# Gated expert values turned by VectorE and memory instead of TensorE, and a peeled step in a new order

## The reference, cut to what matters

```python
# x: (64 sequences, 64 heads, 1024 samples), float32; lengths and languages: one number for each sequence
mask = arange(1024) < length[:, None]
kernel = 2 * real(einsum('hn,hnl->hl', Cs, exp(dtA[:, :, None] * arange(1024))))   # a filter for each head
y = irfft(rfft(x * mask, 2048) * rfft(kernel, 2048))[..., :1024]                   # causal convolution
x = x + (y + x * mask * D[:, None]) * mask

base = einsum('btd,od->bto', x, W)                       # d = o = 1024; t is the head, b the sequence
logits = einsum('btd,ed->bte', x, Wr) + 5 * one_hot(language)       # 8 experts
topw, topi = top_k(logits, 2); gates = softmax weights of the two, put at their experts
h = einsum('btd,erd->bter', x, A)                        # rank 16: 8 x 16 = 128 values for each token
x = x + base + 2 * einsum('bter,bte,eor->bto', h, gates, B)
```

## Time and profile before

| | |
|---|---|
| median of 3 runs (lowest to highest) | 632.15 us (630.82 to 632.97) |
| the profiled execution's own time, its span | 630.64 us, 628.5 us |
| mean granted clock of TensorE | 0.994 |
| TensorE busy | 606.0 us (96%), 3383 matmuls |
| VectorE busy | 525.1 us (84%) |
| ScalarE busy | 447.7 us (71%) |
| DMA, share of 16 engines | 41.6% |

### The profile page before, as it was taken

One profiled execution on the slowest core, in us unless ns is written; L12 is line 12 of the kernel. 1 busy time (PEld: TensorE's weight loads), 2 busy tenths in 40 slices (PEclk: granted clock), 3 DMA queues, 4 the chain that ended last, 5 costly groups with the idle time before them and its releaser, 6 DMA issues.

```text
span 628.5 us, 12633 instructions
## 1 busy us (share of the span) xinstructions
PE 606.0 (96%) x3383; PEld 585.0 (93%) x3383; DVE 525.1 (84%) x1502; ACT 447.7 (71%) x962; POOL 25.2 (4%) x75
## 2 busy tenths in 40 slices
PE   4698989999999999999999999999999999999997
PEld 4597989999999999999999999999999999999997
DVE  7888769888898988888898988889898888988731
ACT  4889688786786867777786778678686877855511
POOL 2341000000000000000000000000000000000000
PEclk9899989999999999999999999999999999999999
DMA  5631443444344444433454444334534444342012
GB/s 182 173 108 34 77 84 69 89 88 77 69 80 92 75 75 88 87 72 69 85 92 70 81 87 86 69 72 87 92 63 87 86 79 76 70 90 60 10 38 63
DMA packets 175936, 50.76 MB, mean 81 GB/s; under 512 B 158216, under 2 KB 170288, under 8 KB 175920
## 3 DMA queue, kind: packets, MB, share of 16 engines
q1 hardware_dynamic: 175840, 50.47, 41.6%
q10 hardware_dynamic: 80, 0.10, 0.0%
HBM read 30.02 MB, written 20.52 MB: 80 GB/s over the span
## 4 chain that ended last, share of the span: by engine, by line
PE 90%; DVE 4%; ACT 4%; issue 1%; POOL 1%; DMA 0%; SPq 0%; DVEq 0%
PE pmg L1399 63%; PE pc L1334 12%; PE pmg L1386 7%; PE px L1334 6%; DVE state L1049 1%; PE pmg L1410 1%; ACT swapped L605 1%; ACT w_hi L511 1%; ACT y_hi L633 0%; DMA logs<-in_L_cond_log_A_real 0%; PE px L1327 0%; DVE w_lo L946 0%; ACT z_swap L540 0%; POOL angle L458 0%; POOL angle L460 0%
## 5 line engine op out<-in xcount | busy, mean ns | idle before, releaser
L1399 PE MATMUL pmg<-w_hi,y_hi 128*128 128x384 f32 (+1 forms) x768 | 261.8, 341 | 1.9 <-DVE y_lo L1097 1.9
L1399 PE MATMUL pmg<-w_lo,y_hi 128*128 128x384 f32 (+1 forms) x768 | 260.3, 339 | 0.0
L1399 PE MATMUL pmg<-w_hi,y_lo 128*128 128x384 f32 (+1 forms) x768 | 260.3, 339 | 0.0
L1399 PEld LDWEIGHTS pmg<-w_hi,y_hi 128*128 128x128 f32 x768 | 144.7, 188 | 2.9 <-issue 2.4
L1399 PEld LDWEIGHTS pmg<-w_hi,y_lo 128*128 128x128 f32 x768 | 144.7, 188 | 0.5
L1399 PEld LDWEIGHTS pmg<-w_lo,y_hi 128*128 128x128 f32 x768 | 144.7, 188 | 0.0
L605 ACT ACTIVATE swapped<-state 64x128 f32<-64x128 f32 (+1 forms) x256 | 92.9, 363 | 50.6 <-DVE state L1049 47.3
L1049 DVE SCALAR_TENSOR_TENSOR state<-swapped,scan_tab,state 128x192 f32<-128x192 f32 (+1 forms) x240 | 73.8, 349 | 18.2 <-ACT swapped L605 10.8
L1049 DVE SCALAR_TENSOR_TENSOR state<-state,scan_tab 128x64 f32<-128x64 f32 x180 | 51.1, 325 | 2.1
L613 ACT ACTIVATE state<-px 128x512 f32<-128x512 f32 x32 | 19.1, 597 | 43.7 <-PE px L1334 43.7
L1097 DVE TENSOR_TENSOR y_lo<-xt,y_hi 128x1024 fp32r<-128x1024 f32 x32 | 39.2, 1225 | 7.0 <-ACT y_hi L633 6.5
(11 more groups left out here) (216 smaller groups left out, 951.7 us busy)
## 6 DMA issues: line engine op xcount, KB each, us to landing
out<-result SPq DMA_DIRECT2D x62, 256.0 KB, 3.1
rows<-in_x SPq DMA_DIRECT2D x224, 64.0 KB, 3.2
toe<-kpad SPq DMA_DIRECT2D x30, 128.0 KB, 4.0
z_store<-Z SPq DMA_DIRECT2D x28, 128.0 KB, 2.1
b_rows<-z_store SPq DMA_DIRECT2D x112, 32.0 KB, 1.8
rows<-in_x SPq DMA_DIRECT2D x8, 256.0 KB, 3.8
rows<-in_L_cond_W SPq DMA_DIRECT2D x3, 512.0 KB, 6.2
result<-in_L_cond_W SPq DMA_DIRECT2D x3, 512.0 KB, 6.1
```

Of the source, the lines that this page charges most:

```text
L1399: ins = nc.tensor.matmul(pm[:, n, 0:o1 - o0], y[s][:, c, :], w[:, c, o0:o1], start=(c == 0 and y is y_hi and w is w_hi), stop=(c == CH - 1 ...
```

## The change

The 128 gated values of each token have to lie with the 128 values on partitions before the LoRA matmuls. Until now TensorE transposes them into PSUM. In the changed kernel VectorE turns them in 32x32 blocks (turn_gated, behind gated and ahead of turn_rows), SyncE stores the blocks to memory in four DMAs that put them in their places (store_gates) and loads the tile back (load_gates, between the fourth and the fifth load of rows). ScalarE and VectorE make gt_hi and gt_lo from that tile, behind y_hi and ahead of y_lo. TensorE runs all 24 matmuls of bank 1 and then all nine of the LoRA. On ScalarE one swap_odd now stands ahead of the evacuations. This holds for 29 steps; (0, 0), (0, 1) and the last one keep turn_gates.

Apart from that, pair 3's rows are loaded as blocks and turned by VectorE, and peeled step (0, 1) has a new order on TensorE, VectorE and ScalarE.

```diff
+    gate_store = nc.dram_tensor("gate_store", (P, P), F32, kind="Internal").ap()
+        gate_blocks = b_rows[:, 4, :, :].rearrange("p o r -> p (o r)")
+        gt = b_rows[:, 5, :, :].rearrange("p o r -> p (o r)")
...
@@ SyncE
-            load_rows(0, 3)
+            load_blocks(0, 3)
...
+            def store_gates(b, m):
+                sp.wait_ge(gates_turned, 2 * b + (m - 1))
+                for k in range(P // SQUARE):
+                    sp.dma_start(bass.AP(gate_store.tensor, k * SQUARE, [[P, SQUARE], [SQUARE * P, P // SQUARE], [1, SQUARE]]),
+                                 gate_blocks[k * SQUARE:(k + 1) * SQUARE, :].rearrange("p (e t) -> p e t", t=SQUARE)
+                                 ).then_inc(gates_stored, 16)
+            def load_gates(b, m):
+                sp.wait_ge(gates_stored, 128 * b + 64 * (m - 1))
+                sp.dma_start(gt, gate_store[:, :]).then_inc(gates_in, 16)
...
             def step(b, m, rows_left=True, first=False):
+                if not first:
+                    store_gates(b, m)
                 if rows_left:
                     sp.wait_ge(xt_ready, 2 * b + m + 3)
-                    load_blocks(b, m + 4)
+                    load_blocks(b, m + 4, range(0, 2))
+                if not first:
+                    load_gates(b, m)
+                if rows_left:
+                    load_blocks(b, m + 4, range(2, 4))
                 block_powers(b, m + 3, first)
...
-            sp.wait_ge(px_full, 4)
+            sp.wait_ge(xt_ready, 4)
             load_blocks(0, 5)
...
@@ ScalarE
+            def split_gates(b, m):
+                act.wait_ge(gates_in, 32 * b + 16 * (m - 1))
+                nc.scalar.activation(gt_hi[:, :], gt, ACT.Copy).then_inc(gthi_ready, 1)
...
-            for n in range(3):
-                swap_odd(0, 2, n)
+            swap_odd(0, 2, 0)
+            waves(2)
+            swap_odd(0, 2, 1)
+            split_turned(0, 3)
+            swap_odd(0, 2, 2)
+            nc.scalar.activation(warm[:, :], phase[:, 0:1], ACT.Exp)
+            ratios(0, 1)
             split_states(0, 2)
-            ratios(0, 1)
-            waves(2)
             split_toe(0, 2)
+            swap_powers(2)
             split_gated(0, 1)
-            split_rows(0, 3)
-            swap_powers(2)
             turn_powers(2, False)
+            split_y(0, 2)
+            copy_states(0, 3)
             evacuate(0, 1, 0)
             evacuate(0, 1, 1)
-            copy_states(0, 3)
-            split_y(0, 2)
-            nc.scalar.activation(warm[:, :], phase[:, 0:1], ACT.Exp)
...
                 if rows_left:
                     split_turned(b, m + 2)
-                split_gated(b, m)
...
                 split_y(b, m + 1)
+                split_gates(b, m)
+                if rows_left:
+                    swap_odd(b, m + 2, 0)
                 for j in range(2):
                     evacuate(b, m, j)
                 if rows_left:
-                    for n in range(3):
-                        swap_odd(b, m + 2, n)
+                    swap_odd(b, m + 2, 1)
+                    swap_odd(b, m + 2, 2)
...
@@ VectorE
+            def turn_gated(b, m):
+                dve.wait_ge(gated_ready, 2 * b + m + 1)
+                vec.transpose(gate_blocks, gated[:, :, :].rearrange("p e r -> p (e r)")).then_inc(gates_turned, 1)
+            def split_gates(b, m):
+                dve.wait_ge(gthi_ready, 2 * b + m + 1)
+                vec.tensor_tensor(gt_lo[:, :], gt, gt_hi[:, :].bitcast(F32), ALU.subtract).then_inc(gtlo_ready, 1)
...
             split_obs(0, 2)
+            turn_rows(0, 3)
...
             route(0, 1)
+            powers(2)
+            split_toe(0, 2)
             split_states(0, 2)
-            split_toe(0, 2)
-            powers(2)
-            split_gated(0, 1)
             split_rows(0, 3)
-            merge(0, 2)
             rotate_pair(2, 0, [gen_scalar(CC_IM, 2, h, False) for h in range(2)])
-            scanning = scan_states(0, 3)
-            next(scanning)
+            merge(0, 2, partial(split_gated, 0, 1))
             split_y(0, 2)
-            for _ in scanning:
+            for _ in scan_states(0, 3):
                 pass
...
                     route(b, m, partial(kernel_column, m + 2), late)
+                    turn_gated(b, m)
                     turn_rows(b, m + 2)
...
-                merge(b, m + 1, partial(split_gated, b, m))
+                merge(b, m + 1)
...
+                split_gates(b, m)
                 split_y(b, m + 1)
...
@@ TensorE
             project(0, 1, 0)
-            turn_rows(0, 3)
             project(0, 1, 1)
             project(0, 1, 2, 0, 4)
             turn_gates(0, 1, 4)
             convolve(0, 2)
+            control(0, 3, alone=True)
+            project(0, 1, 2, 4, 6)
             add_loras(0, 1)
-            control(0, 3)
-            project(0, 1, 2, 4, 8)
+            project(0, 1, 2, 6, 8)
             add_lora(BANK_ORDER[2])
...
                 project(b, m, 1)
-                turn_gates(b, m)
                 convolve(b, m + 1)
                 if rows_left:
                     control(b, m + 2, alone=True)
-                project(b, m, 2, 0, 3)
+                project(b, m, 2)
                 add_loras(b, m)
-                project(b, m, 2, 3, 8)
                 add_lora(BANK_ORDER[2])
```

More of the change, by code:

```diff
@@ L237, in cond_resid_kernel @@
         z2_turned, z_stored, z_blocks_in, ct_ready = sem("z2_turned"), sem("z_stored"), sem("z_blocks_in"), sem("ct_ready")
+        gates_turned, gates_stored, gates_in = sem("gates_turned"), sem("gates_stored"), sem("gates_in")
         second_staged, evens_ready = sem("second_staged"), sem("evens_ready")
@@ L246, in cond_resid_kernel @@
         START = 16
-        TURNED_BY_PE = 64
+        FIRST_LOADS = (64, 32 + 16 * 8)
         BLOCK_LOADS = 16 * 8
@@ L269, in load_rows, with load_blocks @@
                                  ).then_inc(rows_in[s], 16)
-            def load_blocks(b, m):
+            def load_blocks(b, m, groups=range(P // SQUARE)):
                 i, s = 2 * b + m, m % 2
-                for k in range(P // SQUARE):
+                for k in groups:
                     for d in range(SEQS // SQUARE):
@@ L406, in _ @@
             step(LOOPS, 0, rows_left=False)
+            store_gates(LOOPS, 1)
+            load_gates(LOOPS, 1)
             store_result(LOOPS, 1)
+            store_gates(LOOPS + 1, 0)
+            load_gates(LOOPS + 1, 0)
             store_result(LOOPS + 1, 0)
@@ L638, in ratios, with split_gated @@
                                      ).then_inc(ratio_ready, 1)
-            def split_gated(b, m):
-                act.wait_ge(gt_full, 2 * b + m + 1)
+            def split_gated(b, m, turned=None):
+                act.wait_ge(gt_full, 2 * b + m + 1 if turned is None else turned)
                 nc.scalar.activation(gt_hi[:, :], pg[:, 0:P], ACT.Copy).then_inc(gthi_ready, 1)
+            def split_gates(b, m):
+                act.wait_ge(gates_in, 32 * b + 16 * (m - 1))
+                nc.scalar.activation(gt_hi[:, :], gt, ACT.Copy).then_inc(gthi_ready, 1)
             def evacuate(b, m, j):
@@ L806, in _ @@
             ratios(LOOPS + 1, 1)
-            split_gated(LOOPS + 1, 1)
+            split_gated(LOOPS + 1, 1, turned=3)
             for j in range(3):
@@ L960, in turn_rows @@
                 i, s = 2 * b + m, m % 2
-                dve.wait_ge(rows_in[s], TURNED_BY_PE + BLOCK_LOADS * (b + m // 2 - 1))
+                dve.wait_ge(rows_in[s], FIRST_LOADS[s] + BLOCK_LOADS * (b + m // 2 - 1))
                 dve.wait_ge(ylo_ready, i - 1)
```

## The result

The changed kernel takes **648.57 us** (median of 4 runs, 647.24 to 652.92) where the kernel before, run beside it, takes 632.56: a ratio of 1.028, 95% interval 1.0244 to 1.0315. The profiled execution has a span of 646.3 us (before 628.5), 17.8 more, at a mean granted clock of 0.995. I had put 642.0 and 630 to 653: the direction and the range hold, the sum is 6.6 us too low, and the narrower range that I gave the forecast itself, 636 to 648, is missed by 0.6.

The account below looks back on a forecast made before the run. TensorE looked always busy, but VectorE's chain to control arrived with no slack in m = 1. Loop +13.5, peeled steps behind +0.3 and peeled step -2.4 gave +11.4 on 630.64: 642.0 us, range 630 to 653, the forecast's own 636 to 648.

Parts of the forecast that it names:

- turn_gated +0.34 on the chain: VectorE between gated and turn_rows: the added instruction makes turn_rows start 0.34 us later, bounds +0.20 and +0.47.
- the -0.10 of relief: TensorE, each of 29 steps: dropping the transpose of gated saves 0.10 us, -2.9 us at most.
- m = 1 +0.82: Loop's m = 1 steps: 0.48 lateness at turn_blocks plus turn_gated's 0.34 delay u_lo, which has no slack: +0.82 us.
- no cost taken, but no cover left: Step's end: swap_odd(1) and (2) behind evacuations awaiting the LoRA, ready within about 0.1 us of VectorE's scan; nothing charged.
- gt_lo's 0.37 on y_lo: Step's end: y_lo waits for gt_hi, then gt_lo, 0.37 us later against u_lo, delaying the scan and next turn_blocks.
- E's delay: From the experiments, not the prediction: swap_odd(1), behind evacuations that wait for the LoRA, holds the scan; turn_blocks at T+2.9.
- The signs: Expected in the trace: turn_rows 0.34 later, control gaps about 0.3 and 0.8, TensorE idle about 1.2, turn_blocks T+2.9, clock 1.00.
- 13 x 1.04 = 13.5 in the loop: All 13 loop passes: each longer by 0.22 (m = 0) plus 0.82 (m = 1), +13.5 us.
- just in time: Gate values through memory: loaded as ScalarE reaches gt_hi, 3.0 us after load_gates; bound 0 to 0.5 us late.
- Rival (c): Gates land late before gt_hi, delaying evacuations and swaps, or z blocks do: +10, 651 us; chance 0.14.
- The peeled step -2.4: Before the loop: start at 85.5 and slow clock gone save 3.5, late control gives back 1.1, net -2.4 us.
- Peeled steps behind +0.3: Three peeled steps after the loop: +0.22, +0.17 and -0.10, together +0.3 us.

Follow-up runs that it names:

- e4: Kernel before with turn_gated added on VectorE, its result unused and TensorE's transpose kept: 638.63 us, ratio 1.0106.
- e9: Changed kernel without memory trip and gt_lo (gt_hi stands in), swap_odd(1) moved between the two evacuations: 637.88 us, ratio 1.0109.
- e11: Whole changed kernel with swap_odd(1) moved between the two evacuations: 646.51 us, ratio 1.0238 to the kernel before.
- e12: Kernel before with the LoRA matmuls at the step's end and the changed kernel's swap_odd order on ScalarE: 637.69 us, ratio 1.0095.
- e7: Changed kernel without the gate values' memory trip and without gt_lo (gt_hi stands in): 644.60 us, ratio 1.0198 to the kernel before.
- e1: Changed kernel without the gate values' stores and load, splits reading VectorE's blocks directly: 647.45 us, ratio 1.0239 to the kernel before.
- e8: Kernel before with only pair 3's rows as blocks and the new order of peeled step (0, 1): 629.98 us, ratio 0.9982.
- e5: Changed kernel, unaltered, run again on another chip: 649.29 us, ratio 1.0284 to the kernel before.
- e10: Repeat on another chip of the changed kernel without turn_gated, memory trip kept: 644.74 us, ratio 1.0226 to the kernel before.
- e6: Changed kernel without both the gate values' memory trip and turn_gated: 635.32 us, ratio 1.0053 to the kernel before.
- e2: Changed kernel without turn_gated, values stored unturned, memory trip kept: 654.32 us, ratio 1.0347 to the kernel before.
- e3: Changed kernel without gt_lo (gt_hi used twice), memory trip kept: 655.28 us, ratio 1.0362 to the kernel before.

## Why the prediction was right, and where its sum was short

- **The bound.** Right. The busy share said TensorE and nothing else; the hand-measured slack said that VectorE's chain arrives on the dot. e4 shows it: the chain was lengthened by one instruction, and in m = 1, where the slack was zero, the whole of it came through (0.34), in m = 0 0.22.
- **turn_gated +0.34 on the chain.** Right (0.35 in the trace). m = 0: +0.22 predicted with the relief taken off, +0.28 measured. The 0.06 more is lateness of turn_blocks that I took as absorbed: with turn_blocks back at T+2.4 (e9) m = 0 is 18.24, and 18.23 still at T+2.79 (e11), so T+2.90 is just past what is absorbed. In e4 the transpose was still on TensorE, so that run has the delay without the relief, and yet 18.24: the -0.10 of relief changes nothing as long as VectorE sets the step. The two prices that the prediction takes from the Trainium skill are given there for bf16, which it doesn't say; the rows here are float32 (0.31 for the 128x128 turn).
- **m = 1 +0.82.** Right in size (+0.78), wrong in its cause, and so in part luck. The step that failed is the one that called the evacuations and swap_odd "no cost taken, but no cover left" and let gt_lo's 0.37 on y_lo set turn_blocks. What the runs put there: 0.34 from the turn (e4) and 0.47 from the LoRA at the end (e12), together 0.81. The 0.37 itself was about right (turn_blocks at T+2.79 and T+2.83 in e11, T+2.86 predicted) but runs in parallel with E's delay, so the two don't add, and taking gt_lo out alone gains nothing (e7). I had the schedule within 0.1 us on both sides and took the better side of it: the number came out because the two ways end within 0.1 us of each other. "No cover left" was the true reading.
- **The signs.** turn_blocks at T+2.9, half_sum behind the ratio and the clock of 1.00 came as forecast. turn_rows starts 3.15 behind logits instead of 2.72, 0.43 later and not 0.34: 0.35 of it is turn_gated. Of the gap in m = 1 I had expected all at control, put down to u_lo; most of it shows at convolve's second half, put down to s_lo, one instruction earlier in the same chain. And TensorE's rows show 0.45 of idle time in a pass, not 1.2, though the pass is 1.04 longer: rows that overlap hide the rest.
- **13 x 1.04 = 13.5 in the loop.** For passes 2 to 13 that is 12.5; undisturbed they have 13.0 (e1), and as run 15.75.
- **Gate values through memory: "just in time".** Too good, by 2.8 us in passes 2 to 13 (448.29 less e1's 445.50). Rival (c) had the mechanism, ScalarE waiting in front of gt_hi with the swaps behind it, and z blocks late; it had the size wrong, since it struck nine of 24 steps (six with a wait that the rows show), not all. A mean landing time can't tell this. The four stores took 1.74 (1.5 predicted), and I had the load leave at T+12.6 where it left at T+13.25 (177.17 - 163.92), and z_store at T+15.4 where it left at T+15.92.
- **The peeled step -2.4.** Too good, by about as much as the trip. The loop starts at 86.41, not 85.5, and up to T(2,0) the changed kernel is 1.52 behind before, where -2.4 and 1.04 for the first pass would have it 1.36 ahead. Of this 2.9 us, 0.9 is the later start, 1.1 is step (1,0), 20.41 where 18.24 + 1.1 was expected (e8 has it alone: 20.07 against 18.02, 2.05 given back), and 0.9 is step (1,1), 19.78 instead of 18.84, with gt_hi and turn_blocks waiting for their DMAs (0.73 and 0.54). The mechanism was right: the 1.88 wait went, and the slow clock behind it. But this execution has a granted clock of 0.50 from 54.3 to 57.7 us, where the kernel before has 1.00 behind nearly the same two waits (1.42 and 0.64 us of TensorE here, 1.39 and 0.64 before). In e5, e9, e10 and e11, which have the same peeled steps and no such dip, the loop starts at 86.26, 85.64, 85.86 and 85.80, so most of the 0.9 may be that dip; no run shows it apart.
- **Peeled steps behind +0.3.** Measured +0.56.

The difference closes: 17.8 - 11.4 = 6.4 is 2.9 (start and first pass), 3.3 (passes 2 to 13) and 0.3 (peeled steps behind).

By parts, for passes 2 to 13: turn_gated 6.6 (e4), LoRA at the end 5.5 (e12), the trip 2.8 (e1), and 0.9 from their joint effect, mostly in m = 0. The relief of 0.10 a step shows only in e6 and e10, whose m = 0 steps are 17.98 and 17.97, 0.04 and 0.05 below before. Why a DMA lands late in just those steps isn't settled. Nor did I try the gate trip on another queue than SP's.

No version that I ran beats the kernel before by more than the 0.3% that I can tell from no change; e8 comes nearest, and its gain is the peeled step's alone.

## What to carry to other kernels

When the bounding engine is "busy all the time", measure the slack of every chain that feeds it, from the end of the last instruction to the start of its consumer; where it is zero, moving work off the bounding engine onto that chain's engine costs its full length (e4's m = 1 steps, 0.34 us). Moving a consumer to the end of a step moves everything that stands behind it in program order on the engine that drains it: list what is queued behind, and take "within 0.1" as late. And before sending a value through memory, add up the round of the queue that carries it, waits included: near the length of a step it is a second bound, which shows once the first is gone or transfers land late.

## What the runs showed of the hardware that I had not expected

TensorE's matmul rows can hide a slowdown altogether. The same stretch, 125 to 555 us, before and in e4, which runs the same matmuls in steps 1.6% longer:

```profile
125.00:555.00 430.00, 430.00 (x2388) 418.44 (x2387) 379.50 (x1063) 324.20 (x705) 6.74 (x35) 1.00 0.45 81
```
```profile
125.00:555.00 430.00, 430.00 (x2354) 409.23 (x2354) 381.93 (x1078) 320.48 (x698) 6.79 (x35) 1.00 0.44 79
```

TensorE is "busy 430.00" in both, and in e4 no matmul shows a wait; but 2354 matmuls run instead of 2388, and the weight loads are busy 95.2% instead of 97.3%. Matmuls overlap in the rows (in the earlier trace rows one of 0.34 us starts 0.17 before the next), and a gap shorter than the overlap leaves no trace. Perfetto Trace Analysis of the Trainium skill, Identifying the Most-Contended Engine, says that matmul busy time is a poor measure and the weight loads' busy share a better one; here the trace agrees.

The other surprise is e2. With its chain 0.33 us shorter it was 2.9 us slower than the changed kernel over passes 2 to 13 (451.14 against 448.29), and on another chip (e10) 2.3 us faster (445.96). e3, on e2's chip, took 454.96 where e7, without the trip, took 445.32. The changed kernel's two runs differed by 0.2. So a kernel whose queue round is as long as its step takes the landing times of the moment into its own.
